# A Gram product per sample in strips of 32 array columns: four strips and 27 streamed columns in place of two halves and 54

## The chip, the cores and the metric

The kernel runs on one core of one Trainium2 chip, written against the engines directly (no scheduler: every wait is in the code). The metric is the device time of one execution in microseconds (us); lower is better. "PE" is TensorE, "PEld" its weight loads, "ACT" ScalarE, "DVE" VectorE, "POOL" GpSimd, "SP" SyncE, which here issues most DMAs.

## The reference

A recommendation tower over 2048 samples. 27 embedding rows of 128 numbers are looked up per sample, all pairs of them are multiplied (the Gram matrix of the sample, upper triangle without the diagonal, 351 numbers), and a small network follows.

```
e = stack([tbl_f[ids[:, f]] for f in range(27)], axis=1)          # 2048 x 27 x 128
z = einsum('bnd,bmd->bnm', e, e)[:, i, j]                         # i, j = triu_indices(27, k=1)
h = concatenate([z.reshape(2048, -1), dense_ctx], axis=1)         # 351 + 16
h = maximum(h @ W_top1 + b_top1, 0)                               # 512
h = maximum(h @ W_top2 + b_top2, 0)                               # 256
y = h @ W_top3                                                    # 1
```

## The kernel before

The batch is cut into eight pairs of 256 samples (`PAIRS`), each of two tiles of 128 samples. For a pair `p`, and in this order on TensorE (its program is the function at lines 564 to 721):

1. **Look-ups of small tables.** Eleven features with 1000 rows are looked up by one-hot matmuls (`look_up`, lines 572 and 574, a high and a low half of the table). VectorE builds the one-hot operands (line 747). Most look-ups serve two pairs at once.
2. **Turns of gathered rows.** The other sixteen features are fetched by GpSimd: one indirect DMA for each feature and tile (line 543), 32 for a pair and 256 in all, each of 128 rows of 512 bytes. Four features make a bank; TensorE transposes a bank (`turn(p, t, n)`, line 583, four transposes) once its four gathers have landed, and ScalarE copies it into `emb` (line 871). GpSimd holds some gathers back by waits on TensorE's progress (`keep_back`, lines 484 to 530).
3. **Layer 1 of the pair before** (`layer1(p-1, m)`, line 617, four parts `m`), each part followed by one turn of the pair's second tile, `turn(p, 1, m)`. So the last turn of a pair is the one on the critical last gathers of that pair.
4. **Gram products** (`gram_products(p, t)`, lines 588 to 603, the matmul is at line 600): for the first tile, then **layer 2 of the pair before** (`layer2`, line 626), then for the second tile. In the last pair the first tile's products come earlier, after part `m = 1` of layer 1.

The Gram products write banks of PSUM; ScalarE copies each bank into `gram` (`take_gram`, line 882). SyncE stores `gram` to DRAM when a pair is done (`store_products`, line 376) and loads it back in another order as `z` (`load_z`, line 415) for layer 1, one pair later. For the last pair this is done tile by tile (`store_position` at line 334, `load_tile_z` at line 404), and TensorE ends with `layer2(LAST - 1)`, `last_layers(0)` and `last_layers(1)` (lines 644 to 655) and one small transpose (line 720).

In a Gram product before, two samples stand side by side: 54 columns are the stationary operand and the same 54 columns are streamed, so that the two samples' own 27x27 blocks lie on the diagonal of the 54x54 result and the other two blocks are not used. Two such matmuls, one in the lower and one in the upper 64 columns of the array (`HALVES = 2`), make a group of four samples. A tile of 128 samples is 32 groups, 64 matmuls. As the operands are 4-byte floats, each matmul appears in the trace as two records of PE and two of PEld, so 128 of each for a tile and 2048 for the kernel. A bank of PSUM holds eight groups; a tile fills four banks, with two banks in turn.

`gram` also serves at the start as a staging area for three of the small tables (`stages`, line 234), before the first Gram product.

Of the kernel before, what the change touches and what calls it, by code (L numbers as in the profile page):

```python
# [37 lines left out]
P = 128  # L38
BATCH = 2048
NF = 27  # L40
DIM = 128
# [10 lines left out]
ROWS = 125  # L52
ROWS_PER = VOCAB_ONEHOT // ROWS
# [70 lines left out]

HALVES, ABREAST = 2, 2
QUARTERS = HALVES * ABREAST
GROUPS = P // QUARTERS
GRAM_COLS = ABREAST * NF  # L130
HALF_ROWS = P // HALVES
GRAM_PART = HALF_ROWS + GRAM_COLS
GROUPS_A_BANK = 8
GRAM_BANKS = 2
TILE_GRAMS = GROUPS // GROUPS_A_BANK
PAIR_GRAMS = TILES * TILE_GRAMS
RUN = TILES * GROUPS
# [10 lines left out]
STORE_ROWS = 32  # L148
# [4 lines left out]
STAGES = 4  # L153
# [33 lines left out]
def build(nc, dense_t, ids_rows, ids_onehot, gathered_tables, onehot_tables, w1, w2, w3, b1, b2, out):  # L187
    with ExitStack() as ctx:
        def sb(name, shape, dt=F32):
            return ctx.enter_context(nc.sbuf_tensor(name, shape, dt))  # L190
# [8 lines left out]
        ids_b = sb("ids_b", [P, IDS_SLOTS, TILES * PAIR], I32)  # L199
        rows = sb("rows", [P, TILES, NG, DIM])  # L200
        emb = sb("emb", [P, TILES, P, NF])
        gram = sb("gram", [P, ABREAST, NF, RUN])
        z = sb("z", [P, STEPS, PAIR])
        table_hi = sb("table_hi", [P, NO, ROWS_PER, DIM], F32R)
        table_lo = sb("table_lo", [P, NO, ROWS_PER, DIM], F32R)
# [20 lines left out]

        products = nc.dram_tensor("products", (2, DRAM_ROWS, NF, QUARTERS, RUN), F32)

        last_products = nc.dram_tensor("last_products", (TILES, DRAM_ROWS, NF, QUARTERS, GROUPS), F32)


        part = ROWS_PER * DIM
        gram_flat = gram[:, :, :, :].rearrange("p s j g -> p (s j g)")
        stages = [gram_flat[0:ROWS, k * part:(k + 1) * part] for k in range(STAGES - 1)]
        stages.append(h1[0:ROWS, :, :].rearrange("p m b -> p (m b)"))


# [8 lines left out]
        gram_ps = [bank(f"gram_ps{i}") for i in range(GRAM_BANKS)]  # L246
# [36 lines left out]
        gram_taken = sem("gram_taken")  # L283
# [22 lines left out]

        def stored_rows(q):

            half, s = divmod(q, ABREAST)
            row = half * HALF_ROWS + s * NF  # L310

            pad = PAD if q == QUARTERS - 1 else 0
            return row - pad, row - pad + STORE_ROWS, PAD - pad
# [18 lines left out]
        def store_position(engine, t, q):  # L332
            row, end, to = stored_rows(q)
            engine.dma_start(last_products[t, to:to + STORE_ROWS, :, q, :],
                             gram[row:end, q % ABREAST, :, t * GROUPS:(t + 1) * GROUPS]
                             ).then_inc(last_products_out[t], 16)

        block = ctx.enter_context(nc.Block())
# [2 lines left out]
        def _(sp):  # L341
# [29 lines left out]
            def store_products(p):  # L371

                sp.wait_ge(gram_taken, (p + 1) * PAIR_GRAMS)
                for q in range(QUARTERS):
                    row, end, to = stored_rows(q)
                    sp.dma_start(products[p % 2, to:to + STORE_ROWS, :, q, :], gram[row:end, q % ABREAST, :, :]  # L376
                                 ).then_inc(products_out, 16)

            def entries(p, step):
# [5 lines left out]
            def store_tile(t):  # L385

                sp.wait_ge(gram_taken, LAST * PAIR_GRAMS + (t + 1) * TILE_GRAMS)
                for q in range(QUARTERS if t == 0 else QUARTERS // 2):
                    store_position(sp, t, q)
# [159 lines left out]
        def _(pe):  # L549
# [36 lines left out]
            def gram_products(p, t):  # L586

                pe.wait_ge(emb_taken, tile_end(p, t))
                for i in range(TILE_GRAMS):
                    a = p * PAIR_GRAMS + t * TILE_GRAMS + i  # L590
                    if a >= GRAM_BANKS:

                        pe.wait_ge(gram_taken, a - GRAM_BANKS + 1)
                    ps = gram_ps[a % GRAM_BANKS]
                    for b in range(GROUPS_A_BANK):
                        group = i * GROUPS_A_BANK + b
                        for half in range(HALVES):
                            first = group * QUARTERS + half * ABREAST
                            samples = emb[:, t, first:first + ABREAST, :].rearrange("d s f -> d (s f)")
                            last = nc.tensor.matmul(  # L600
                                ps[half * HALF_ROWS:half * HALF_ROWS + GRAM_COLS, b * GRAM_COLS:(b + 1) * GRAM_COLS],
                                samples, samples, start=True, stop=True)
                    last.then_inc(gram_full, 1)

            def layer1(p, m):
# [203 lines left out]
        def _(act):  # L809
# [64 lines left out]
            def take_gram(p, t):  # L874
                if t == 0 and p > 0:

                    act.wait_ge(products_out, p * QUARTERS * 16)
                for i in range(TILE_GRAMS):
                    a = p * PAIR_GRAMS + t * TILE_GRAMS + i
                    act.wait_ge(gram_full, a + 1)  # L880
                    g0 = t * GROUPS + i * GROUPS_A_BANK
                    nc.scalar.copy(  # L882
                        gram[0:GRAM_PART, :, :, g0:g0 + GROUPS_A_BANK].rearrange("r s j g -> r (s j) g"),
                        gram_ps[a % GRAM_BANKS][0:GRAM_PART, 0:GROUPS_A_BANK * GRAM_COLS].rearrange(
                            "r (g c) -> r c g", c=GRAM_COLS)).then_inc(gram_taken, 1)

            def take_layer1(chunk, m):
                act.wait_ge(mlp_full, chunk + m + 1)
# [121 lines left out]
```

## Time and profile before

| what | us |
|---|---|
| median of 3 runs (lowest, highest) | 348.53 (348.14, 349.94) |
| span of the profiled execution, first to last instruction | 346.3 |
| difference of the two (start and end outside the span) | 2.2 |
| PE busy in the span | 331.1 (96%) |
| POOL busy in the span | 242.9 (70%) |
| DVE busy in the span | 219.4 (63%) |
| ACT busy in the span | 184.7 (53%) |

The profile is of one execution; its times are counted from the first instruction. The page gives for each engine the share of the span in which it was busy, a picture of 40 slices, the costliest groups of instructions, and the chain of work that ended last, followed back from the last instruction. Queries of the trace give the instructions in order of time, the waits, and the counts in chosen stretches. A group "busy" on an engine does not by itself say that the engine sets the time; for that one looks at what each engine waits for.

### The profile page before, as it was taken

Reading aid. Unit: us, or ns where it says so; the run is one execution under the profiler, and the core shown is the slowest. Engines: PE = TensorE matmul, PEld = TensorE weight load, DVE = VectorE, ACT = ScalarE, POOL = GpSimd, SP = SyncE. Lnnn points to the kernel's source line nnn. Section 1 sums busy time; section 2 is a strip of 40 time slices with the busy share of each in tenths; the row PEclk is TensorE's granted clock in tenths of the full one; section 3 lists DMA queues with packets and bytes.
Section 4 is the critical chain, followed back from the end, with each engine's and each line's share of the span. In section 5 each row is a group of like instructions: output and inputs, shape, how many; then the busy total and the mean of one; then the engine's idle time right before and its main releaser. Section 6 shows DMA issues by size and latency. Waiting matters only on the chain.

```text
span 346.3 us, 8212 instructions
## 1 busy us (share of the span) xinstructions
PE 331.1 (96%) x3478; PEld 282.8 (82%) x3478; DVE 219.4 (63%) x160; ACT 184.7 (53%) x315; POOL 242.9 (70%) x263
## 2 busy tenths in 40 slices
PE   2899999999999999999999999999999999998995
PEld 1667878887898888887898889887888889997894
DVE  5899997599427971499626991399724990360021
ACT  4898975533646354633646355633447346554521
POOL 6777777777777777777777777777777777777200
PEclk9999999999999999999999999999999999999999
DMA  6975795655237772768229772677327552572440
GB/s 169 222 178 168 225 252 142 156 157 135 67 55 157 146 158 55 107 173 178 83 55 157 146 160 55 89 197 177 83 57 134 131 112 57 85 168 72 85 81 8
DMA packets 53981, 44.06 MB, mean 127 GB/s; under 512 B 39810, under 2 KB 43983, under 8 KB 53945
## 3 DMA queue, kind: packets, MB, share of 16 engines
q1 hardware_dynamic: 43993, 26.52, 35.1%
q0 software_dynamic: 8192, 16.79, 21.3%
q8 instruction: 28, 0.46, 0.6%
q10 hardware_dynamic: 1760, 0.22, 0.4%
q14 instruction: 8, 0.07, 0.1%
HBM read 36.43 MB, written 7.09 MB: 126 GB/s over the span
## 4 chain that ended last, share of the span: by engine, by line
PE 86%; DMA 6%; SPq 3%; ACT 2%; issue 1%; DVE 1%; DVEq 0%
PE emb_ps L572 21%; PE emb_ps L574 20%; PE gram_ps L600 16%; PE mlp_ps L617 11%; PE mlp_ps L626 7%; PE emb_ps L583 7%; DMA h<-tbl_rows 3%; DMA products<-gram 1%; DMA gram<-tbl_rows 1%; PE emb_ps L644 1%; SPq L376 1%; DMA z<-products 1%; SPq L369 1%; PE mlp_ps L671 1%; PE mlp_ps L655 1%
## 5 line engine op out<-in xcount | busy, mean ns | idle before, releaser
L543 POOL DMA_INDIRECT rows<-tbl_rows,idx x256 | 242.0, 945 | 78.9 <-issue 74.4
L747 DVE TENSOR_TENSOR onehot<-ids_b,row_id 125x2048 fp32r<-125x2048 int32 x72 | 158.9, 2279 | 33.3 <-PE emb_ps L574 33.3
L572 PE MATMUL emb_ps<-onehot,table_hi 125*128 125x512 f32 (+1 forms) x400 | 147.6, 378 | 5.6 <-DVE table_lo L768 4.0
L574 PE MATMUL emb_ps<-onehot,table_lo 125*128 125x512 f32 (+1 forms) x400 | 143.0, 367 | 0.0
L572 PEld LDWEIGHTS emb_ps<-onehot,table_hi 125*128 125x128 f32 x400 | 76.0, 190 | 21.5 <-DVE table_lo L768 4.8
L574 PEld LDWEIGHTS emb_ps<-onehot,table_lo 125*128 125x128 f32 x400 | 76.1, 190 | 10.7
L600 PEld LDWEIGHTS gram_ps<-emb 128*54 128x54 f32 x2048 | 53.6, 130 | 5.6 <-issue 3.5
L600 PE MATMUL gram_ps<-emb 128*54 128x54 f32 x2048 | 55.8, 214 | 1.7 <-ACT emb L852 0.8
L851 ACT COPY held<-emb_ps 128x256 f32<-128x256 f32 x38 | 14.1, 371 | 75.9 <-PE emb_ps L574 75.8
L784 DVE TENSOR_TENSOR mlp_ps<-mlp_ps,rows 128x256 f32<-128x256 f32 x14 | 6.1, 433 | 76.5 <-PE mlp_ps L626 76.5
L882 ACT COPY gram<-gram_ps 118x432 f32<-118x432 f32 x64 | 33.2, 519 | 39.5 <-PE gram_ps L600 39.2
L871 ACT COPY emb<-emb_ps 128x512 f32<-128x512 f32 x64 | 45.5, 710 | 0.0
L617 PE MATMUL mlp_ps<-z,w_sb 126*128 126x256 f32 x168 | 41.2, 380 | 1.0 <-DMA z<-products 1.0
L583 PE MATMUL emb_ps<-ident,rows 128*128 128x128 f32 x256 | 38.8, 274 | 0.0
L852 ACT COPY emb<-emb_ps 128x256 f32<-128x256 f32 x50 | 34.4, 688 | 7.9 <-PE emb_ps L574 7.9
L583 PEld LDWEIGHTS emb_ps<-ident,rows 128*128 128x128 f32 x256 | 31.0, 140 | 7.2 <-issue 0.5
L747 DVE TENSOR_TENSOR onehot<-z,mlp_ps 125x2048 fp32r<-125x2048 int32 (+1 forms) x16 | 33.5, 2114 | 2.0 <-PE mlp_ps L671 1.3
L617 PEld LDWEIGHTS mlp_ps<-z,w_sb 126*128 126x128 f32 x168 | 30.1, 190 | 4.7 <-DMA z<-products 1.2
L626 PE MATMUL mlp_ps<-w_sb,h 128*128 128x256 f32 x112 | 26.0, 386 | 0.0
L626 PEld LDWEIGHTS mlp_ps<-w_sb,h 128*128 128x128 f32 x112 | 20.7, 190 | 2.9
L891 ACT ACTIVATE h<-mlp_ps,columns 128x256 f32<-128x256 f32 x28 | 13.3, 474 | 17.6 <-PE mlp_ps L617 17.6
L862 ACT COPY emb<-held 128x1280 f32<-128x1280 f32 (+1 forms) x7 | 19.2, 2741 | 0.2
(49 smaller groups left out, 102.6 us busy)
## 6 DMA issues: line engine op xcount, KB each, us to landing
ids_b<-ids_onehot SPq DMA_DIRECT2D x33, 256.0 KB, 5.5
products<-gram SPq DMA_DIRECT2D x28, 216.0 KB
gram<-tbl_rows SPq DMA_DIRECT2D x9, 480.0 KB
rows<-tbl_rows,idx POOLq DMA_INDIRECT x256, 2.9
z<-products SPq DMA_DIRECT2D x14, 126.0 KB
h<-tbl_rows SPq DMA_DIRECT2D x2, 480.0 KB
z<-products SPq DMA_DIRECT2D x7, 112.0 KB
w_sb<-w SPq DMA_DIRECT2D x1, 768.0 KB, 5.8
```

The source lines that it names most:

```text
L543: pool.indirect_dma_start(out=rows[:, t, f, :], out_offset=None, in_=gathered_tables[f], in_offset=bass.IndirectOffsetOnAxis(ap=idx[:, p, ...
L572: nc.tensor.matmul(ps[:, 0:width], table_hi[0:ROWS, k, j, :], columns[:, c, :], start=j == 0, stop=False)
L574: last = nc.tensor.matmul(ps[:, 0:width], table_lo[0:ROWS, k, j, :], columns[:, c, :], start=False, stop=j == ROWS_PER - 1)
L583: last = nc.tensor.transpose(ps[:, f * P:(f + 1) * P], rows[:, t, first + f, :], ident[:])
L600: last = nc.tensor.matmul(ps[half * HALF_ROWS:half * HALF_ROWS + GRAM_COLS, b * GRAM_COLS:(b + 1) * GRAM_COLS], samples, samples, start=Tr ...
L617: last = nc.tensor.matmul(ps[:, 0:PAIR], w1_sb[0:k, s, m * P:(m + 1) * P], z[0:k, s, :], start=s == 0, stop=s == STEPS - 1)
L626: last = nc.tensor.matmul(mlp_ps[t][:, 0:HID2], h1[:, k, t * P:(t + 1) * P], w2_sb[:, k, :], start=k == 0, stop=k == M1 - 1)
L747: nc.vector.tensor_tensor(onehot[0:ROWS, seq % ONEHOT_RING, 0:own * width].rearrange("p (j b) -> p j b", b=width), *operands, ALU.is_equal ...
L852: nc.scalar.copy(emb[:, :, :, NG + k], ps[:, 0:PAIR].rearrange("d (t b) -> d t b", t=TILES)).then_inc(emb_taken, 1)
L862: nc.scalar.copy(emb[:, :, :, slot:slot + size].rearrange("d t b f -> d (t b) f"), held[:, 0:size, :].rearrange("d f b -> d b f")).then_in ...
L871: nc.scalar.copy(emb[:, t, :, first:first + size], ps[:, 0:size * P].rearrange("d (f b) -> d b f", f=size)).then_inc(emb_taken, 1)
L882: nc.scalar.copy(gram[0:GRAM_PART, :, :, g0:g0 + GROUPS_A_BANK].rearrange("r s j g -> r (s j) g"), gram_ps[a % GRAM_BANKS][0:GRAM_PART, 0: ...
```

## The change

Each sample gets a matmul of its own: 27 columns are the stationary operand and 27 are streamed. Four samples of a group lie in four strips of the array of 32 columns each (rows 0, 32, 64 and 96 of the PSUM bank). A tile is 32 groups, 128 matmuls in place of 64; a bank holds sixteen groups in place of eight, so a tile fills two banks in place of four. ScalarE makes two copies for a tile in place of four, each of 432 numbers in a partition as before. `gram` loses its dimension of two samples abreast and becomes a view of a separate staging buffer `stage`; the four stores of a pair take their 32 rows from partitions 0, 32, 64 and 91 on. GpSimd's, VectorE's and SyncE's programs keep their order; their waits on the count of filled or taken Gram banks use the new number of banks for a tile.

```diff
-HALVES, ABREAST = 2, 2
-QUARTERS = HALVES * ABREAST
+STRIPS, STRIP_ROWS = 4, 32
+QUARTERS = STRIPS
 GROUPS = P // QUARTERS
-GRAM_COLS = ABREAST * NF
-HALF_ROWS = P // HALVES
-GRAM_PART = HALF_ROWS + GRAM_COLS
-GROUPS_A_BANK = 8
+GRAM_PART = (STRIPS - 1) * STRIP_ROWS + NF
+GROUPS_A_BANK = 16
 GRAM_BANKS = 2
...
-        gram = sb("gram", [P, ABREAST, NF, RUN])
+        stage = sb("stage", [P, STAGES - 1, ROWS_PER * DIM])
+        gram = stage[:, :, :].rearrange("p k c -> p (k c)")[:, 0:NF * RUN].rearrange("p (j g) -> p j g", j=NF)
...
-        gram_flat = gram[:, :, :, :].rearrange("p s j g -> p (s j g)")
-        stages = [gram_flat[0:ROWS, k * part:(k + 1) * part] for k in range(STAGES - 1)]
+        stages = [stage[0:ROWS, k, :] for k in range(STAGES - 1)]
...
         def stored_rows(q):
-            half, s = divmod(q, ABREAST)
-            row = half * HALF_ROWS + s * NF
+            row = q * STRIP_ROWS
...
                     for b in range(GROUPS_A_BANK):
                         group = i * GROUPS_A_BANK + b
-                        for half in range(HALVES):
-                            first = group * QUARTERS + half * ABREAST
-                            samples = emb[:, t, first:first + ABREAST, :].rearrange("d s f -> d (s f)")
-                            last = nc.tensor.matmul(
-                                ps[half * HALF_ROWS:half * HALF_ROWS + GRAM_COLS, b * GRAM_COLS:(b + 1) * GRAM_COLS],
-                                samples, samples, start=True, stop=True)
+                        for strip in range(STRIPS):
+                            sample = emb[:, t, group * QUARTERS + strip, :]
+                            row = strip * STRIP_ROWS
+                            last = nc.tensor.matmul(ps[row:row + NF, b * NF:(b + 1) * NF], sample, sample,
+                                                    start=True, stop=True)
                     last.then_inc(gram_full, 1)
...
                     nc.scalar.copy(
-                        gram[0:GRAM_PART, :, :, g0:g0 + GROUPS_A_BANK].rearrange("r s j g -> r (s j) g"),
-                        gram_ps[a % GRAM_BANKS][0:GRAM_PART, 0:GROUPS_A_BANK * GRAM_COLS].rearrange(
-                            "r (g c) -> r c g", c=GRAM_COLS)).then_inc(gram_taken, 1)
+                        gram[0:GRAM_PART, :, g0:g0 + GROUPS_A_BANK],
+                        gram_ps[a % GRAM_BANKS][0:GRAM_PART, 0:GROUPS_A_BANK * NF].rearrange(
+                            "r (g c) -> r c g", c=NF)).then_inc(gram_taken, 1)
```

## Rows read from the trace of the kernel before

**Rows 1.** The page: busy time and share; 40 slices of PE, POOL.

```profile
PE 331.1 (96%) x3478; PEld 282.8 (82%) x3478; DVE 219.4 (63%) x160; ACT 184.7 (53%) x315; POOL 242.9 (70%) x263
...
PE   2899999999999999999999999999999999998995
...
POOL 6777777777777777777777777777777777777200
```

**Rows 2.** The page's groups: count, busy us, mean ns, idle before and releaser.

```profile
L600 PE MATMUL gram_ps<-emb 128*54 128x54 f32 x2048 | 55.8, 214 | 1.7 <-ACT emb L852 0.8
...
L882 ACT COPY gram<-gram_ps 118x432 f32<-118x432 f32 x64 | 33.2, 519 | 39.5 <-PE gram_ps L600 39.2 <-issue 0.3
```

**Rows 3.** PE's waits from 64 to 343 us: total, times, longest (us).

```profile
PE mlp_ps L617 <- DMA z<-products: 1.0, 1, 1.0
PE gram_ps L600 <- ACT emb L871: 0.7, 1, 0.7
```

**Rows 4.** One line, the gathers: ns min/median/max, first and last start; landing.

```profile
L543 POOL DMA_INDIRECT rows<-tbl_rows,idx x256: 940/945/1097, 2.8 to 321.6; - x128
...
DMA to landing us min/median/max: 2.4/2.9/4.6
```

**Rows 5.** POOL's last two gathers in order of time: start, us, what, idle before.

```profile
320.35 0.94 POOL L543 DMA_INDIRECT rows<-tbl_rows,idx  x1 [0.30 <-issue]
321.59 0.94 POOL L543 DMA_INDIRECT rows<-tbl_rows,idx  x1 [0.30 <-issue]
```

**Rows 6.** The chain that ended last, first tiles of three pairs: start, us, what.

```profile
210.06 3.42 PE gram_ps L600 x128
...
251.64 3.42 PE gram_ps L600 x128
...
289.21 3.42 PE gram_ps L600 x128
```

**Rows 7.** The same chain, its end.

```profile
322.72 0.44 PE emb_ps L583 x4
323.16 1.31 PE mlp_ps L617 x6
...
324.98 0.66 ACT emb L871
...
325.69 3.44 PE gram_ps L600 x128
329.13 3.65 PE mlp_ps L626 x16
...
337.62 0.67 PE emb_ps L644 x6
...
343.46 0.26 ACT dense L960
```

**Rows 8.** Timeline near the end: the last turn; tile 0's stores and loads.

```profile
321.81 2.74 SPq L334 DMA_DIRECT2D last_products<-gram  x4
...
324.32 0.63 PE L583 MATMUL emb_ps<-ident,rows 128*128 128x128 f32 x4
...
326.78 3.08 SPq L404 DMA_DIRECT2D z<-last_products  x3
```

**Rows 9.** A Gram tile's start: us, PE busy (matmuls in flight), PEclk, DMA, GB/s.

```profile
93.37:93.39 0.02, 0.02 (x4) 1.00 1.14 205
93.39:93.42 0.03, 0.03 (x4) 1.00 0.48 137
93.42:93.44 0.02, 0.02 (x6) 1.00 3.12 614
```

**Rows 10.** PE in order of time, the first look-up's 512-column matmuls.

```profile
9.51 0.80 PE L572 MATMUL emb_ps<-onehot,table_hi 125*128 125x512 f32 x1 [4.03 <-DVE table_lo L768]
...
12.66 0.59 PE L574 MATMUL emb_ps<-onehot,table_lo 125*128 125x512 f32 x1
13.09 0.40 PE L572 MATMUL emb_ps<-onehot,table_hi 125*128 125x512 f32 x1
13.32 0.40 PE L574 MATMUL emb_ps<-onehot,table_lo 125*128 125x512 f32 x1
```

More of the change, by code:

```diff
@@ L334, in store_position @@
             engine.dma_start(last_products[t, to:to + STORE_ROWS, :, q, :],
-                             gram[row:end, q % ABREAST, :, t * GROUPS:(t + 1) * GROUPS]
+                             gram[row:end, :, t * GROUPS:(t + 1) * GROUPS]
                              ).then_inc(last_products_out[t], 16)
@@ L375, in store_products @@
                     row, end, to = stored_rows(q)
-                    sp.dma_start(products[p % 2, to:to + STORE_ROWS, :, q, :], gram[row:end, q % ABREAST, :, :]
+                    sp.dma_start(products[p % 2, to:to + STORE_ROWS, :, q, :], gram[row:end, :, :]
                                  ).then_inc(products_out, 16)
```

## The prediction

> **What bounds the kernel now.** Three views, in this order. The page's busy shares first: PE has 96% and nine tenths or more in nearly every slice, so TensorE looks like the bound, and the Gram products at L600 are 55.8 us of it [rows 1, 2]. The waits of PE agree at first sight: from 64 to 343 us it waited twice, 1.7 us in all [rows 3].
>
> Then the gathers, because the POOL row of the slices is oddly even: a 7 in every slice from the second to the 37th, whatever the other engines do [rows 1]. The line of the gathers explains it: 256 of them, started from 2.8 to 321.6 us [rows 4]. (321.6 - 2.8) / 255 = 1.250 us from one start to the next, and the last two, which follow each other without a wait, have the same spacing: 0.94 busy and 0.30 between [rows 5]. A mean over the whole kernel that equals the spacing of two unhindered neighbours leaves no room for a wait in between. So GpSimd issues gathers back to back from the first to the last, and its 70% is 0.945 of every 1.25 us; the holds of `keep_back` had always come true in time. POOL is a second bound, hidden by its share.
>
> Which of the two sets the end? A pair needs 32 gathers, 32 x 1.25 = 40.0 us on POOL. On PE the pairs' first Gram tiles start at 210.06, 251.64 and 289.21, that is 41.6 and 37.6 us apart, 39.6 on average [rows 6]: the two streams run at the same pace. At the end they meet. The last gather starts at 321.59 and lands 2.4 to 2.9 us later (shortest, median), so at 324.0 to 324.5 [rows 4, 5]; the turn that needs it starts at 324.32 [rows 8]. PE never waits for a gather, but there it is no more than about 0.3 us behind one. From there the chain is all on PE and ACT: copy of the turn 0.66, Gram of the last tile 3.44, layer 2 3.65, last layers, end at 346.3 [rows 7].
>
> So a faster PE before 324 us is worth nothing: it will wait for gathers. Only what the change saves behind the last turn counts.
>
> **The change, part by part.** *The last tile's Gram, on the path.* It takes 3.44 us now, 128 records [rows 7], 26.9 ns for each. The records come in pairs: four in flight from 93.37 to 93.42, six from 93.42 on, two new ones within a stretch of 20 ns and none in the 30 ns before [rows 9]. Two halves of the array work at the same time, each at one record of 54 columns in some 53.4 ns (3.42 us / 64) [rows 6]. After: 256 records of 27 columns in four strips, 64 for a strip. The trace has no strip of 32, so bounds from the nearest rows. Lower: a record costs half of 53.4, four strips abreast: 64 x 26.7 ns = 1.71 us. Upper: nothing but the count matters and each record keeps its 26.9: 256 x 26.9 = 6.9 us. Between: a fixed part that doesn't shrink. Four transposes of 128 columns take 0.44 us, 110 ns each [rows 7], against 53.4 for 54 columns: (110 - 53.4) / 74 = 0.76 ns a column, which leaves 32.8 ns for 27 columns and 64 x 32.8 = 2.1 us. I take 1.9, between 1.71 and 2.1, because rows 9 show that records in different parts of the array don't queue behind each other. Saved on the path: 3.44 - 1.9 = 1.5 us (1.3 to 1.7).
>
> The Trainium skill speaks against this choice: "TensorEngine Tiling (Array Packing)", section "Instruction Overhead", puts about 60 cycles on every matmul, gives one of 1 column the time of one of 60, and advises not to take the tiling factor from a dimension that is already small. By it a record would cost 27 columns as much as 54 and the doubled count would decide; that is the third rival below. For the pair that rows 9 show, the trace does not agree that this cost is the whole engine's, since two records begin together; no run here shows four strips.
>
> *The other fifteen tiles.* 15 x 1.5 = 22 us less work of PE. They come back as waits of PE at the turns (L583), since the gathers keep their 1.25 us: 0 on the path. PE now needs 39.6 us a pair and then about 36.6, against POOL's 40.0.
>
> *The turn and its copy.* The turn cannot start before 324.0 to 324.5, and starts at 324.32 now: -0.3 to +0.2, I take 0.
>
> *ACT's copies* at L882: 32 in place of 64 of the same 432 numbers, 32 x 519 ns = 16.6 us less on an engine that is 53% busy [rows 1, 2]; the last copy of a tile still follows its last matmul by one copy, so 0 on the path. With two banks for a tile the wait for a free bank moves to the next tile, 3.65 us of layer 2 later [rows 7] against 0.52 for a copy: hidden. If that cover were gone (pair 0, where both tiles follow each other), a copy's 0.5 us would be late at 55 us, far ahead of the gathers' end.
>
> *The staging buffer, the stores, the waits on bank counts:* same loads, same bytes and numbers of DMAs, same places in the queues of SP and POOL; 0. The PE program grows by 2 x 2048 records; its fetching is a DMA of its own, and I put a stall of it with the third rival.
>
> *What moves.* In the last pair PE will run ahead and stand at the turns. The second last bank's gathers land 5.0 us before the last (four gathers), so at 319.0 to 319.5; turn 0.44, layer 1 1.31, free at 320.8 to 321.2; then about 3.2 us of waiting. The first tile's Gram comes earlier too, and with it its stores (now 321.81) and its loads of z (now 326.78) [rows 8], by about 4 us; the loads then run beside the last gathers. -0 to +2.1 us, the bound being the spread of the landing, 4.6 against 2.5 [rows 4]; I take +0.1.
>
> **Sum.** 346.3 - 1.5 + 0.1 = 344.9 of span. The median of the runs stands 2.2 us above the span: 347.1, 0.4% less than 348.53. About 0.5%, 1.7 us, is what a measurement of this kernel can tell from no change; so I forecast "same", on its fast edge. This case's own range is 346.3 to 347.9.
>
> **Rivals.** *1. TensorE's clock falls in the new waits.* The granted clock reads 1.00 in the Gram tile [rows 9]. But the first look-up, after 4.03 us of idle, has its 512-column matmuls 0.43 us apart up to 13.09 and 0.23 from there [rows 10]: 512 / 0.43 is the 1.2 GHz level, later 2.4, and it rose after 3.6 us of uninterrupted matmuls. The longest wait in the run since was 1.0 us, without a fall [rows 3]; mine is some 3.2, and after it come only 0.44 of transposes and ACT's 0.66 before the Gram. At 1.2 GHz the turn costs some 0.2 more, the Gram about 1.5 more, and layer 2 the rest until it rises: +2.0, so 349.1. For it: no row shows 3.2 us of waiting that left the clock up. Against it: 3.2 is shorter than the 4.03 of the only row.
>
> *2. The last gathers land late*, because z's loads now meet them: the landing at its worst, +2.1, 349.2. Against it: in the rows of before the stores of the first tile are issued at the same time as the last gather, and its turn started at 324.32 all the same [rows 8].
>
> *3. Slower: every record costs the engine its time, whatever the strips and columns.* The place is L600, in all sixteen tiles. At 26.9 ns a tile takes 6.9 us in place of 3.44, 3.45 more; PE, then clearly slower than POOL, is the bound, and 16 x 3.45 = 55 gives 404. It decides from 13.4 ns a record on: below that a tile is shorter than now, at 15 ns it is 0.4 us longer and 6 us are lost. Fetching twice the instructions, 512 records a tile, would act alike. For it: 26.9 a record is what the trace has. Against it: the pairs of rows 9.
>
> *4. The strips don't work side by side as the change says*, or only two of them: the tile stays near 3.4 us and the time at 348.5.
>
> *5. The first reading: PE is the bound and every tile counts.* 16 x 1.5 = 24 us, 324.5. Against it: the gathers alone last until 324 us, and 22 us of chain stand behind them. It could only be if gathers came faster with a less busy PE, and their 1.25 us is the same in busy slices and at the edges.
>
> **How the numbers follow.** Forecast 0.49, clock 0.21, late gathers 0.11, cost per record 0.08, no gain 0.07, all tiles 0.04. The predicted time is the forecast's 347.1. The range: below the forecast's 346.3 lie the last case and a little of the first; above, the clock (349.1) and late gathers (349.2) with 0.8 for their own spread must be in, so 346.2 to 350.0; the cost per record stays out. Faster by over 0.5% means below 346.8: a third of the forecast, 0.16, and the last case, 0.04: 0.20. Slower means above 350.3: 0.08, and 0.05 from the upper ends of clock and gathers: 0.13. Same: 0.67.
>
> **What will show it.** Right: a Gram tile near 1.9 us (x256); the gathers' line again from 2.8 to 321.6 with 940/945; waits of PE at L583 for rows, some 20 us where there were none; PE's share near 90%; the last tile's Gram starting near 325.7 and layer 2 near 327.6. Wrong on the clock: a granted clock under 1.00 after 321 us, and 128-column transposes over 110 ns apart. Wrong on gathers: the last turn after 324.6. Wrong on strips: a tile at 3.4 us or more. Wrong altogether: the last gather's start moving from 321.6.

## The result and the profile after

The kernel after takes 394.07 us (median of 4 runs, 390.94 to 399.11) against 348.78 (4 runs, 348.14 to 349.94). Two of its four runs were disturbed; without them the ratio is 1.121 (95% interval 1.117 to 1.125). The prediction said 347.1 in a range of 346.2 to 350.0: it was wrong, and on the other side. The profiled execution is the one of 390.94 us; its span is 388.8, 42.5 more than the 346.3 before.

The page of the kernel after, lines that answer [rows 1], with the granted clock, the share of "issue" in the chain and the instruction queue (packets, MB, share):

```profile
PE 343.9 (88%) x5526; PEld 285.8 (74%) x5526; DVE 219.6 (56%) x160; ACT 167.8 (43%) x283; POOL 243.1 (63%) x263
...
PE   2999984799988998799988997899988998898787
...
PEclk9999996699989998789999999899998999999899
...
q8 instruction: 44, 0.72, 0.8%
...
PE 80%; issue 9%; DMA 6%; SPq 2%; ACT 1%; DVE 1%; DVEq 0%
```

The last two of these lines in the page of the kernel before:

```profile
q8 instruction: 28, 0.46, 0.6%
...
PE 86%; DMA 6%; SPq 3%; ACT 2%; issue 1%; DVE 1%; DVEq 0%
```

PE has dents, though it is the bound now. "Issue" is time in which the chain's engine waited for nothing that the profile shows: 9% of 388.8 is some 35 us, and before it was 1%. The page's groups (count, busy us, mean ns, idle before) say where; they answer [rows 2, 4]:

```profile
L540 POOL DMA_INDIRECT rows<-tbl_rows,idx x256 | 242.3, 947 | 108.2 <-issue 70.9
...
L597 PE MATMUL gram_ps<-emb 128*27 128x27 f32 x4096 | 57.2, 197 | 30.4 <-issue 25.5
L597 PEld LDWEIGHTS gram_ps<-emb 128*27 128x27 f32 x4096 | 47.4, 107 | 41.7 <-issue 37.5
...
L878 ACT COPY stage<-gram_ps 123x432 f32<-123x432 f32 x32 | 16.6, 520 | 93.5 <-PE gram_ps L597 93.5
```

The Gram line has as much busy time as before (57.2 against 55.8) for twice the records, and beside it 30.4 us of idle time, 25.5 of them with nothing as the releaser. POOL's gathers, which ran without a break before, now wait, and the last one starts at 351.1 us instead of 321.6 [rows 4, 5]:

```profile
L540 POOL DMA_INDIRECT rows<-tbl_rows,idx x256: 942/947/1100, 2.7 to 351.1; - x128
```

Inside a tile, the chain of waits from 103 to 112 us (start, us, what), which answers [rows 6]:

```profile
103.73 0.89 PE gram_ps L597 x54
104.62 0.09 issue
104.71 0.70 PE gram_ps L597 x31
105.41 0.07 issue
105.48 0.40 PE gram_ps L597 x13
105.88 0.08 issue
105.96 0.69 PE gram_ps L597 x30
106.65 1.80 issue
108.45 0.66 PE gram_ps L597 x46
109.11 3.06 PE mlp_ps L622 x7
```

The records run in quick bursts and stop: shortly at 104.6, 105.4 and 105.9, then for 1.8 us at 106.65, with all operands in place. The tile takes 5.4 us instead of 3.42. The same microseconds on POOL and on the weight loads, in order of time:

```profile
104.07 0.95 POOL L540 DMA_INDIRECT rows<-tbl_rows,idx  x1 [1.78 <-PE emb_ps L580]
105.32 0.95 POOL L540 DMA_INDIRECT rows<-tbl_rows,idx  x1 [0.30 <-issue]
```

```profile
104.71 0.59 PEld L597 LDWEIGHTS gram_ps<-emb 128*27 128x27 f32 x57 [0.20 <-issue]
105.47 0.29 PEld L597 LDWEIGHTS gram_ps<-emb 128*27 128x27 f32 x22 [0.17 <-issue]
105.95 0.59 PEld L597 LDWEIGHTS gram_ps<-emb 128*27 128x27 f32 x55 [0.19 <-issue]
```

The short stops end 0.64 us after a gather's start (104.71), then 0.15 and 0.63 after the next one's (105.47, 105.95). They keep step with the gathers; the long stop doesn't. (Of the 59 gaps of 0.15 to 0.35 us between the starts of neighbouring Gram records in this trace, 54 end 0.13 to 0.18 or 0.62 to 0.65 us after a gather's start.) Last, the granted clock in that tile and in the stretches behind it (us, busy times of five engines, PEclk, DMA share, GB/s):

```profile
103.75:109.10 5.35, 3.31 (x257) 2.76 (x257) 0.00 (x0) 1.20 (x3) 3.81 (x5) 1.00 0.16 40
109.10:112.40 3.30, 3.30 (x10) 2.61 (x10) 0.00 (x0) 1.17 (x2) 2.69 (x3) 0.53 0.27 65
```

The tile itself has the full clock; layer 2 behind it runs near the 1.2 GHz level. Before, the mean clock of the run was 1.000, now it is 0.952.

**Where the 42.5 us are.** From the trace I added up, by kind of work, the time from the first matmul of a stretch of one kind to the first of the next. The columns to the right are experiments told below.

| us | before | after | all quarters spread | pairs 1 to 6 spread | pairs 1 to 6 whole | one pass |
|---|---|---|---|---|---|---|
| Gram products | 55.0 | 86.2 | 66.5 | 56.2 | 76.8 | 34.1 |
| look-ups | 171.2 | 176.4 | 173.0 | 173.6 | 174.6 | 175.3 |
| turns | 29.6 | 30.0 | 31.6 | 31.2 | 29.6 | 31.7 |
| layer 1 | 36.6 | 37.9 | 39.7 | 38.4 | 36.5 | 48.9 |
| layer 2 | 25.5 | 29.9 | 29.0 | 27.3 | 27.0 | 27.4 |
| spreading of the ids, at the start | 10.5 | 11.3 | 11.4 | 10.7 | 11.2 | 12.1 |
| span | 346.3 | 388.8 | 369.1 | 354.7 | 373.6 | 346.6 |
| mean granted clock | 1.000 | 0.952 | 0.972 | 1.000 | 0.982 | 0.961 |

The last layers, not in the table, take 10.8 us in each of the six. After against before: Gram +31.2; everything else +12.2, most of it in look-ups (+5.2) and layer 2 (+4.4), whose instructions the change doesn't touch and which run partly at the lower clock. Together that is 43.4 for the span's 42.5 (what follows the last matmul is 0.9 us shorter). So the question is what stops a Gram tile 1 to 2 us long.

### The profile page after: what moved, and what is told of

It reads as the page before. It is cut to its first block, busy times and chain, and to the rows that moved or that the text cites. A ratio compares the mean times of both kernels' runs of the same rounds, so it can differ in the third digit from the quotient of the medians.

```text
span 388.8 us, 12276 instructions
## 1 busy us (share of the span) xinstructions
PE 343.9 (88%) x5526; PEld 285.8 (74%) x5526; DVE 219.6 (56%) x160; ACT 167.8 (43%) x283; POOL 243.1 (63%) x263
## 4 chain that ended last, share of the span: by engine, by line
PE 80%; issue 9%; DMA 6%; SPq 2%; ACT 1%; DVE 1%; DVEq 0%
PE emb_ps L569 20%; PE emb_ps L571 19%; PE gram_ps L597 15%; PE mlp_ps L613 10%; PE mlp_ps L622 8%; PE emb_ps L580 6%; DMA h<-tbl_rows 3%; DMA stage<-tbl_rows 1%; DMA z<-products 1%; DMA products<-stage 1%; PE emb_ps L640 1%; SPq L373 1%; SPq L366 1%; PE mlp_ps L667 0%; PE mlp_ps L651 0%
## 5 line engine op out<-in xcount | busy, mean ns | idle before, releaser
L569 PE MATMUL emb_ps<-onehot,table_hi 125*128 125x512 f32 (+1 forms) x400 | 151.0, 387 | 6.5 <-DVE table_lo L764 4.4
L571 PE MATMUL emb_ps<-onehot,table_lo 125*128 125x512 f32 (+1 forms) x400 | 146.3, 375 | 0.0
L569 PEld LDWEIGHTS emb_ps<-onehot,table_hi 125*128 125x128 f32 x400 | 78.3, 196 | 22.6 <-DVE table_lo L764 5.1
L571 PEld LDWEIGHTS emb_ps<-onehot,table_lo 125*128 125x128 f32 x400 | 78.4, 196 | 11.5
L597 PE MATMUL gram_ps<-emb 128*27 128x27 f32 x4096 | 57.2, 197 | 30.4 <-issue 25.5
L597 PEld LDWEIGHTS gram_ps<-emb 128*27 128x27 f32 x4096 | 47.4, 107 | 41.7 <-issue 37.5
L878 ACT COPY stage<-gram_ps 123x432 f32<-123x432 f32 x32 | 16.6, 520 | 93.5 <-PE gram_ps L597 93.5
L613 PE MATMUL mlp_ps<-z,w_sb 126*128 126x256 f32 x168 | 42.5, 389 | 1.0 <-DMA z<-products 1.0
L622 PE MATMUL mlp_ps<-w_sb,h 128*128 128x256 f32 x112 | 30.5, 433 | 0.9 <-issue 0.9
L622 PEld LDWEIGHTS mlp_ps<-w_sb,h 128*128 128x128 f32 x112 | 24.0, 219 | 5.0 <-issue 0.8
```

Source lines behind the costliest of these rows:

```text
L569: nc.tensor.matmul(ps[:, 0:width], table_hi[0:ROWS, k, j, :], columns[:, c, :], start=j == 0, stop=False)
L571: last = nc.tensor.matmul(ps[:, 0:width], table_lo[0:ROWS, k, j, :], columns[:, c, :], start=False, stop=j == ROWS_PER - 1)
L597: last = nc.tensor.matmul(ps[row:row + NF, b * NF:(b + 1) * NF], sample, sample, start=True, stop=True)
L613: last = nc.tensor.matmul(ps[:, 0:PAIR], w1_sb[0:k, s, m * P:(m + 1) * P], z[0:k, s, :], start=s == 0, stop=s == STEPS - 1)
L622: last = nc.tensor.matmul(mlp_ps[t][:, 0:HID2], h1[:, k, t * P:(t + 1) * P], w2_sb[:, k, :], start=k == 0, stop=k == M1 - 1)
L878: nc.scalar.copy(gram[0:GRAM_PART, :, g0:g0 + GROUPS_A_BANK], gram_ps[a % GRAM_BANKS][0:GRAM_PART, 0:GROUPS_A_BANK * NF].rearrange("r (g c ...
```

## The experiments

The theory formed on the two traces (S, supply): PE's instructions come by a DMA queue in packets, and strips use them up faster than they come. The instruction queue grew from 28 packets and 0.46 MB to 44 and 0.72 MB for 2 x 2048 more records (a matmul and a weight load each count as one instruction): 0.26 MB / 4096 = 63 bytes an instruction, and 0.72 MB / 44 = 16.4 KB, some 256 instructions, a packet. The rivals: every record costs the engine its time (R), the gathers hinder PE, the strips themselves cost (their clock, the rows of PSUM that they write, or their evictions, which are ScalarE's copies out of PSUM).

**1. Two of four strips.** Half of the Gram products are left out.

```
- for strip in range(STRIPS):
+ for strip in range(STRIPS // 2):
```

> The changed kernel, but only strips 0 and 1 of each group are computed (the Gram products of the other half of the samples are left out), so a tile has 128 matmul records and 256 instructions on TensorE as in the kernel before, each of 27 columns. Theory S (supply: TensorE's instructions arrive in blocks of 256, about 3.1 to 4 us apart at best, and a tile of 512 outruns them): no stop over 0.6 us inside a Gram tile, a tile 1.1 to 1.6 us; TensorE is then faster than the gathers, which run again without extra waits from about 2.8 to 321.6 us, and the end is theirs: span 344 to 346, time 346 to 348. Rival R (every record costs the engine its time, 17 to 20 ns on average in the changed kernel): a tile 2.2 to 2.6 us. Rival C (strips of 27 columns let the clock fall, and that is the loss): granted clock under 1.00 around most Gram tiles, and a time well over 350.

Measured: 347.97 us (346.19 to 350.88, 10 runs), ratio 0.998 (0.995 to 1.001). PE's longest waits and the line of the gathers:

```profile
PE emb_ps L580 <- DMA rows<-tbl_rows,idx: 12.8, 8, 3.1
```

```profile
L540 POOL DMA_INDIRECT rows<-tbl_rows,idx x256: 940/944/1099, 2.8 to 321.3; - x128
```

With 256 instructions a tile, as before, the loss is gone. What PE saves comes back as waits for gathers, 12.8 us at the turns, and the gathers run from 2.8 to 321.3 as in [rows 4]. So the prediction's step that GpSimd sets the end, and that a faster PE before 324 us is worth nothing, holds. The tiles took mostly 1.9 to 2.0 us, more than was expected, and three still had a long stop (3.8 us of "issue" together, the longest 1.6). A tile without a stop took 1.88 us: 64 records for each of two strips, some 29 ns a record.

**2. Empty instructions.** The kernel before, with four `nop("pad", nofuse=True)` behind each Gram matmul.

> The kernel before with four empty instructions behind each Gram matmul: the same matmuls of 54 columns in two halves, but 512 instructions for a tile, as many as the changed kernel has. Theory S: stops of 1 to 2 us at block boundaries inside the Gram tiles, a tile of 4.5 to 5.5 us in place of 3.42, time 365 to 390. Rival R (the cost is that of matmul records): the 128 records are unchanged, a tile stays at 3.4 to 3.6, time within 1% of before. If an empty instruction itself takes long, the records will be evenly further apart instead of stopped at a few places.

Measured: 622.43 us (one run). That is far above what either theory expected. A tile takes about 18 us without a long stop, some 286 ns for a Gram matmul and its four fillers. Less the 53.4 ns that the matmul took before, that leaves some 58 ns for each empty instruction, an estimate from one run at a mean granted clock of 0.771. 512 instructions in 18 us are 36 ns each, and at that pace nothing outruns the supply measured below; the run tells nothing of it.

**3. Gathers of the first pair only.** The kernel after without the gathers of pairs 1 to 7, whose gathered rows are then those of pair 0.

```
- for p in range(PAIRS):          # POOL's gathers
+ for p in range(1):
...
- pe.wait_ge(gathered[t][n], (p + 1) * 16 * size)
+ pe.wait_ge(gathered[t][n], 16 * size)
```

> The changed kernel without the 224 gathers of pairs 1 to 7 (the gathered rows of pair 0 are used again). Theory G for the short stops of about 0.27 us in the Gram tiles (they come with the gathers): none from pair 1 on, as in the last pair of the changed kernel, whose gathers were over. Theory S for the long stops: they stay, 1 to 2.4 us in nearly every tile, a tile 3.8 to 4.6 us in place of 4.4 to 6.7. Time 370 to 385. If the long stops go too, the gathers were what delayed the instructions, and the time falls to about 350.

Measured: 385.31 us (one run). One tile from 100 us on and one from 320 us on, in order of time:

```profile
100.63 1.90 PE L597 MATMUL gram_ps<-emb 128*27 128x27 f32 x201
104.89 0.66 PE L597 MATMUL gram_ps<-emb 128*27 128x27 f32 x55 [2.36 <-issue]
...
320.37 2.36 PE L597 MATMUL gram_ps<-emb 128*27 128x27 f32 x256
324.94 1.44 PE L622 MATMUL mlp_ps<-w_sb,h 128*128 128x256 f32 x3 [2.22 <-issue]
```

The short stops are gone, so they are the gathers' doing; they are worth no more than the some 6 us between the 391 of the profiled execution and 385. The long stops stay, one of 2.0 to 2.8 us in nearly each tile. In the second tile shown, all 256 records run through in 2.36 us and the stop comes right behind the last. R falls: a record in four strips costs 9 ns (2.36 us / 256) when instructions are there, not 26.9. And the time doesn't come down to before's with GpSimd out of the way, so the loss isn't the gathers'.

**4 and 5. The last tile alone in strips; the same, with the program shifted.** The kernel before, its last Gram tile in strips; in 5, 32 matmuls of one column (128 instructions) stand near the start of PE's program.

```
+ def in_strips(p, t):
+     return p == LAST and t == TILES - 1
...
+ pad(12)        # run 5 alone: at the start
...
+ pad(20)        # run 5 alone: ahead of look_up(0)
```

> The kernel before, with only the very last Gram tile (pair 7, second tile) computed in four strips of 27 columns; everything ahead of it as before. Counted in blocks of 256 instructions of TensorE's program, this tile crosses a block boundary after about 77 and again after about 205 of its 256 records. Theory S (supply in blocks, the next one ready 3.1 to 4 us after the boundary ahead of it was crossed): one stop of 1.5 to 2.6 us near record 206, none at 77; the tile 4.0 to 4.8 us in place of 3.44, so 0.6 to 1.4 us more, ratio 1.001 to 1.004. Rival R (a record costs 17 to 20 ns): a tile of 4.4 to 5.1 us, its records evenly apart. Forecast of the prediction (a strip tile takes 1.9): 1.5 us less, ratio 0.996.

> The same as the run with the last tile in strips, plus 32 one-column matmuls at the very start, where TensorE waits for the first tables: 128 instructions more, which move the block boundaries in the last tile to about record 14 and record 142 and into the layer 2 behind it. The first of these is crossed early, while TensorE still waits for the last gather's turn to be copied. Theory S: no stop over 0.6 us inside the last tile, the tile 2.1 to 2.5 us, 0.7 to 1.3 us less than before: ratio 0.996 to 0.998. Rival R: no difference to the run without the shift (tile 4 to 5 us, ratio 1.001 to 1.004).

Measured: 350.72 us (6 runs), ratio 1.007 (1.004 to 1.009), and 350.16 (6 runs), 1.004 (1.002 to 1.007). The last tile in order of time, first in run 4, then in run 5:

```profile
326.12 2.15 PE L606 MATMUL gram_ps<-emb 128*27 128x27 f32 x206 [0.74 <-ACT emb L882]
330.69 0.62 PE L606 MATMUL gram_ps<-emb 128*27 128x27 f32 x50 [2.42 <-issue]
331.24 2.00 PE L637 MATMUL mlp_ps<-w_sb,h 128*128 128x256 f32 x8
```

```profile
325.98 1.49 PE L606 MATMUL gram_ps<-emb 128*27 128x27 f32 x142 [0.74 <-ACT emb L891]
329.41 1.18 PE L606 MATMUL gram_ps<-emb 128*27 128x27 f32 x114 [1.94 <-issue]
330.52 3.05 PE L637 MATMUL mlp_ps<-w_sb,h 128*128 128x256 f32 x7
```

These rows settle it. The tile, its data and its neighbours are the same, and the stop moved from behind record 206 to behind record 142. 64 records of two instructions (a weight load and a matmul) are 128 instructions: the stop sits at a place in the program, and moves exactly with it. No theory of the array, of PSUM or of the gathers puts it there. The distance fits too: where run 3 has two tiles in a row (pair 0), its long stops come behind records 235, 362 and 490, that is 127 and 128 records, 256 instructions, apart. The same tiles stop behind the same records in run 3 and in the kernel after (201, 184, 167 and 151 in pairs 1 and 2). The gain that I expected of 5 did not come. A tile of 512 instructions meets two packet edges wherever it begins, here behind records 14 and 142. I had taken the first to be crossed while PE waits ahead of the tile, so that the packet for the second would be there in time; but the tile began at 325.98, and that packet's DMA started only at 327.04. In 5 the clock fell behind the tile as well (granted clock 0.50 from 330.9 to 334.2; 7 matmuls of layer 2 in 3.05 us against 8 in 2.00).

The instruction DMAs around these stops, from the trace's DMA records: in run 4 one from 327.79 to 329.21, records again at 330.69; in run 5 one from 327.04 to 328.05, records at 329.41; in the kernel after one from 105.55 to 107.01, records at 108.45. So 1.4 to 1.5 us pass from a packet's end to its first instruction. This holds in every trace: of the 68 gaps of over 1 us between the starts of neighbouring records that begin in a Gram tile, 67 end 1.25 to 1.55 us after an instruction packet's DMA ended. The other one, in run 9 at 279.0 us, is left open. Where two strip tiles follow each other without other work (pair 0), a packet (a block of 256 instructions) comes into use every 3.73, 3.55 and 3.73 us in the chain of run 6 (told below), of which this is the part in pair 0:

```profile
58.80 0.85 PE gram_ps L602 x56
...
62.53 2.01 PE gram_ps L602 x112
...
66.08 2.17 PE gram_ps L602 x98
...
69.81 0.50 PE gram_ps L602 x19
```

The same distances are 3.82 and 3.45 us in run 3, 3.82 and 3.73 in run 7, and 4.10 and 4.00 in the kernel after. 256 instructions in 3.45 to 4.10 us are 13.5 to 16.0 ns for each, 27 to 32 for a record. That is the sustained supply. A tile of before uses 256 instructions in 3.42 us [rows 6]: it was already at this edge, and where its two tiles follow each other it had a small stop, as the chain of the kernel before shows:

```profile
54.72 6.51 PE gram_ps L600 x234
61.23 0.24 issue
61.47 0.76 PE gram_ps L600 x21
```

This stop is of the same kind: it stands behind record 234, and the records go on at 61.47, 1.40 us after an instruction packet's DMA ended at 60.07.

The Trainium skill, "Runtime: NRT & Kernel Launch", section "Instruction fetch mechanics", says that an engine's program comes in blocks of 256 instructions by a queue of its own, the next one during the current one; block size and queue agree with the 63 bytes and 16.4 KB above. It also says that the cost of crossing a block is mostly hidden, because instructions are dispatched more slowly than they are filled in. The trace does not agree with that: 512 instructions of a strip tile are used in 2.36 us, 4.6 ns each, and the crossing then costs 2.2 us (run 3, the second tile shown).

**6 and 7. Quarters of a tile spread between other work; the same, shifted.** The kernel after, in pairs 1 to 6 with 64 records behind each turn and 64 ahead of every second k of layer 2; 7 adds the start of 5.

```
  layer1(p - 1, m); turn(p, 1, m)
+ if p < LAST: gram_quarter(p, 0, m)
  ...
+ if beside is not None and k % 2 == 0: gram_quarter(beside, 1, t * 2 + k // 2)
```

> The changed kernel with the same matmuls in another order in pairs 1 to 6: the first tile's Gram products in quarters of 64 records, one behind each turn of layer 1's four parts, the second tile's in quarters between the matmuls of layer 2; pairs 0 and 7 as in the changed kernel. Theory S: the same number of records and instructions no longer outruns the supply, since the long matmuls between them give it 1.3 to 2 us for each 128 instructions; stops of over 0.6 us go in pairs 1 to 6, TensorE keeps ahead of the gathers, which run from 2.8 to about 322 again; the last tile keeps its one stop. Time 347 to 352 in place of 391. Rival R (cost of each record, wherever it stands): over 380. Rival C (narrow strips by themselves let the clock fall): granted clock under 1.00 in most of pairs 1 to 6 and a time of 360 or more.

> The same as the run with spread quarters, plus the 32 one-column matmuls at the start that move the block boundaries in the last tile. Theory S: the last tile's stop goes or shrinks, 1 to 2 us less than the run without: 346 to 349. What is left of the prediction (a strip tile near 2.1 us behind the last gather, about 1.2 us less than before, if the clock stays up) would show here: 347. If the clock falls in the wait for the last gathers, 348 to 350.

Measured: 371.54 us (4 runs), ratio 1.066 (1.063 to 1.069), and 373.40 (4 runs), 1.071 (1.068 to 1.075). Nearly half of the loss is gone, with the same instructions, but both runs missed what was expected (347 to 352 and 346 to 349). The shift gains no time; it moves the stops of pair 0 by 64 records again, from behind 235, 362 and 490 to behind 171, 298 and 426. A spread quarter takes 0.67 to 0.95 us and seldom stops. Of what is left, 10.2 us are where tiles stay whole: pair 0's two take 14.9 us (the stops shown above) in place of 7.4, the last pair's 9.6 in place of 6.8. And 20.5 us pass at the lower clock, in and behind these tiles.

**8 and 9. Only pairs 1 to 6 in strips, spread or whole.** The kernel before, with twelve of its sixteen tiles in strips, banks of eight groups in both, and their stores taken from the strips' rows; 8 spreads the quarters as 6 does, 9 leaves each tile in one piece.

```
+ def in_strips(p, t):
+     return 0 < p < LAST
```

> The kernel before, with pairs 1 to 6 in strips (banks of eight groups, so a quarter tile is 64 records), each quarter put between other work: tile 0's behind the four turns of tile 1, tile 1's between the layer 2 matmuls. Pairs 0 and 7 keep the products of before. Supply theory (a block of 256 PE instructions can be used some 3 to 4 us after the block ahead of it, no sooner): the quarters take the 0.67 to 0.95 us that they took in these pairs of the kernel with all quarters spread, hardly a long stop is left, the clock stays at 1.00, the last gathers start at 321.3 to 323 us, and the time is that of before: 347.5 to 349.5 us. PE saves time in twelve tiles and POOL's gathers give none of it away. Rival (strips themselves cost: the narrow products, the evictions of 27 columns a group, the layout, the clock): what was left of the loss with all quarters spread, 23 us, belongs to 16 tiles, and 12 of them keep their share: 362 to 368 us.

> The same twelve tiles in strips with the same evictions, but each tile in one piece where before has it, 256 records in a row; pairs 0 and 7 as before. Supply theory: each tile meets at least one block boundary that comes too early and stops 1 to 2.5 us there; tiles take 4.4 to 5.4 us instead of 3.42, 12 x 1.0 to 2.0 us, and the clock falls behind some of them: 358 to 374 us. Rival (strips themselves cost): the same time as with the quarters spread, within 3 us.

Measured: spread 357.16 us (4 runs), ratio 1.026 (1.023 to 1.028); whole 376.41 (4 runs), 1.080 (1.075 to 1.086), 2 us above the range expected of it. In order of time, first spread, then whole:

```profile
290.20 0.60 PE L591 MATMUL emb_ps<-ident,rows 128*128 128x128 f32 x4
290.73 0.91 PE L608 MATMUL gram_ps<-emb 128*27 128x27 f32 x64
291.57 1.56 PE L630 MATMUL mlp_ps<-z,w_sb 126*128 126x256 f32 x6
292.97 0.60 PE L591 MATMUL emb_ps<-ident,rows 128*128 128x128 f32 x4
...
301.54 0.55 PE L608 MATMUL gram_ps<-emb 128*27 128x27 f32 x43
302.82 0.36 PE L608 MATMUL gram_ps<-emb 128*27 128x27 f32 x21 [0.73 <-issue]
```

```profile
222.25 3.10 PE L608 MATMUL gram_ps<-emb 128*27 128x27 f32 x212
226.62 0.57 PE L608 MATMUL gram_ps<-emb 128*27 128x27 f32 x44 [1.26 <-issue]
```

The same products, evictions and instructions cost 19 us more in whole tiles than in quarters: the twelve tiles take 62.1 us together against 41.8, and the clock falls behind four of the whole ones and behind none of the quarters. So the strips alone don't lower the clock.

Run 8 was expected at 347.5 to 349.5 and missed by 8 us, and neither theory had it. The table names the place. The quarters' 41.8 us are 3.48 a tile, no less than 3.42: 0.67 when nothing stops them (2.7 a tile), the rest is short stops and some six longer ones like that at 302.1. And each passage between wide matmuls and Gram products costs the wide work beside it: from 290.20 to 290.73 a turn takes 0.53 us where it takes 0.44 ahead of layer 1 [rows 7], and layer 1 from 291.57 to 292.97 takes 1.40 in place of 1.31. This is not the strips' own: in the kernel before, too, a turn ahead of a Gram tile takes 0.53, and the one part of layer 1 that follows a Gram tile 1.40. But spreading adds three more such passages in each of six pairs: 18 x 0.09 = 1.6 us at the turns and 18 x 0.09 = 1.6 in layer 1, and the table has +1.6 and +1.8; layer 2 in four pieces adds 1.8. The look-ups' +2.4 stay unexplained. PE, which had no slack, is longer by the sum. Why a passage costs this tenth was not tried.

**10. One pass.** The kernel after with the embeddings rounded to bfloat16, which changes the Gram products: each is then one weight load and one matmul in place of two and two.

```
- emb = sb("emb", [P, TILES, P, NF])
+ emb = sb("emb", [P, TILES, P, NF], mybir.dt.bfloat16)
```

> The kernel after with the embeddings of the Gram product rounded to bfloat16, which changes that part of the computation: each product is then one weight load and one matmul instead of two and two, with the same strips, the same 2048 products, the same banks and evictions, and PE's program is as long as that of before (7133 instructions against 11229). Supply theory: a tile of 128 records and 256 instructions meets one block boundary and takes 1.1 to 2.2 us with a stop in few of them; the gathers keep their pace of 1.250 us and the time is 346 to 349 us. Rival (four strips at once, their write rows or their evictions cost, whatever the instructions): tiles above 3.5 us, over 370 us.

Measured: 347.70 us (346.47 to 349.70, 10 runs), ratio 0.999 (0.996 to 1.001). One pair's tiles, and PE's longest waits:

```profile
247.03 1.76 PE L597 MATMUL gram_ps<-emb 128*27 128x27 bf16 x128
...
252.37 1.89 PE L597 MATMUL gram_ps<-emb 128*27 128x27 bf16 x128
```

```profile
PE emb_ps L580 <- DMA rows<-tbl_rows,idx: 9.5, 7, 3.1
PE gram_ps L597 <- issue: 4.9, 4, 2.3
```

All four strips, all 2048 products, the same banks and evictions, and as many instructions as before: the loss is gone, so none of these by itself is its cause. Most tiles take 1.7 to 1.9 us. That this is the size that the prediction gave a tile is chance: it was for 256 records, and here there are 128, with two or three short stops in most tiles. It isn't faster than before either, although the Gram products take 34.1 us in place of 55.0: what PE saves turns up as waits for rows at the turns, 9.5 us, and as work at the lower clock. The table has both mostly with layer 1 (36.6 to 48.9), since a stretch there reaches to the first matmul of the next turn. The gathers run to 323.9. None of the variants beat the kernel before; after run 1, with half the products gone and 0.2% at most to show, none could be expected to by this change.

## Why the prediction was wrong

- **What bounds the kernel: right, and not enough.** That GpSimd's gathers hold the end at about 347 us whatever PE saves is shown by runs 1 and 10. But it is a floor for a faster PE only. PE became slower, and in the kernel after POOL waits for PE: the last gather starts at 351.1 instead of 321.6 [rows 5]. With no slack on either side [rows 6], each us that PE loses counts.
- **The last tile, 1.9 us: the mechanism right, the size a little low, and the supply missing.** The strips do work side by side: a record costs 26.9 ns in two halves [rows 7], some 15 in two strips (run 1) and 9 in four (run 3). The tile of run 3 without a stop takes 2.36 us, so some 37 ns for one strip's record, above the 32.8 from which the prediction had its 2.1 us. But the last tile, in strips alone (run 4), took 5.12 us in place of 3.44: the supply added more than the strips saved.
- **The step that failed** is the sentence that the program "grows by 2 x 2048 records; its fetching is a DMA of its own, and I put a stall of it with the third rival". It got no price of its own and no row; it was put beside a rival of 0.08 that rows 9 were held against. What the runs showed in its place: a packet of 256 instructions comes into use every 3.45 to 4.10 us at best, a strip tile needs two packets, and it stops 1 to 2.4 us at an edge, 31.2 us more for the Gram products. The page of before held the means for a price: 28 instruction packets for 6956 matmuls and weight loads, and a tile of 256 instructions in 3.42 us. A form with twice the instructions in 1.9 us asks for 512 in that time, 3.6 times the rate of before's Gram tiles, its densest stretches; no row bounded that from above, and the 0.24 us of "issue" behind record 234 in pair 0 pointed to the limit.
- **The third rival named the right side with the wrong cause, and 0.08 was too little for it.** Its 26.9 ns a record, 6.9 us a tile and 404 us are close, by chance, to what a supply of 27 to 32 ns a record gives where two tiles follow each other (15.1 us for two in the kernel after). A tile between other work passed one of its two edges without a long stop and took 5.1 on average ((86.2 - 15.1) / 14). The pairs of [rows 9], which I held against it, are true and speak of the array, not of the supply. Its "fetching twice the instructions would act alike" is what happened.
- **The Trainium skill's rule** that I weighed ("TensorEngine Tiling (Array Packing)", "Instruction Overhead": some 60 cycles a matmul, don't take the factor from a small dimension) gave the right advice, but the loss did not come by it. The trace agrees in so far as a strip's record of 27 columns costs more than half of one of 54 (37 ns in run 3 against 53.4); it does not agree that the two cost the same, nor that the cost is the whole engine's, at 9 ns a record.
- **The clock rival** came true in another place. The clock was to fall in waits at the turns; in the kernel after there are none, and it fell in and behind Gram tiles. It was low for 37.5 us, and the work other than Gram products took 12.2 us longer, where the rival had put the price at 2; how much of the 12.2 is the clock's was not tried. In run 1 it did what the rival said: after a wait of 2.25 us the last turn took 0.95 us and the last tile 2.6, at a granted clock of 0.50 from 324.1 to 327.3.
- **ACT's copies** went from 64 to 32 and from 33.2 to 16.6 us. Run 10, which has them too and the time of before, shows no cost or gain of them, as forecast. The stores and staging were not tried by themselves.

## What to carry to other kernels

Before packing small matmuls side by side, divide: instructions of a stretch by its hoped-for time, against the densest stretch that the trace has run for several hundred instructions. Here 13.5 to 16 ns an instruction was the sustained limit, two fp32 passes with a weight load each made four instructions a product, and the tuned form already sat at that limit; packing pays only with fewer instructions for each product or with long instructions between them. And look for a second engine that hides just under the first, as GpSimd does here: it decides what is left of the gain.

## What the runs showed of the hardware

- PE's program comes in packets of 256 instructions; a long stop sits at a packet's edge and moves with the program (206 to 142 records for 128 instructions). At these stops a packet came into use 1.25 to 1.55 us after its DMA ended, and one every 3.45 to 4.10 us where tiles of strips followed each other (pair 0).
- A gather on GpSimd held PE's instructions up twice, for about 0.2 us, until about 0.15 and 0.64 us after its start; without gathers these stops were gone (run 3). Beside wide matmuls and the tiles of before they cost nothing: from 100 to 142 us of the kernel before, with gathers all along, PE was busy for 42.00 of 42 us.
- An empty instruction on PE cost some 58 ns, by the estimate of run 2.
- Passing from full-width matmuls to Gram products and back, in strips or in halves, took about 0.1 us each way (0.44 to 0.53, 1.31 to 1.40).
- The clock fell behind tiles with long stops in the kernel after and in run 9, and stayed at 1.00 in run 8 with the same strips in quarters. In run 10 it also fell, mean 0.961, behind waits for rows and for ScalarE's copies among others, and in run 2, mean 0.771, with the halves of before spaced apart. What exactly makes it fall is left open.
